# Last layers of a four-layer cross-attention stack on one Trainium2 core: rows normalised by a three-operand VectorE instruction with the reciprocal deviation as a broadcast tensor, in place of the form with two scalars

## The reference, cut to what matters

```python
def layernorm(x, scale, bias):
    m = jnp.mean(x, axis=-1, keepdims=True)
    v = jnp.mean(jnp.square(x - m), axis=-1, keepdims=True)
    return (x - m) * jax.lax.rsqrt(v + EPS) * scale + bias
ln_out = layernorm(hidden_states, ln1_s, ln1_b)
...                                   # self attention, 16 heads, masked; x = hidden + attn_out
ln_out = layernorm(x, ln2_s, ln2_b)
...                                   # cross attention over the context; x = x + cross_out
ln_out = layernorm(x, ln3_s, ln3_b)
mlp_out = gelu(ln_out @ w1 + b1) @ w2 + b2
return x + mlp_out
```

## Time and profile before

| | |
|---|---|
| median of 3 runs | 1350.19 us (1348.3 to 1353.55) |
| the profiled execution's own time | 1349.58 us |
| its span, first to last instruction | 1347.8 us |
| mean granted TensorE clock | 0.989 |
| PE busy | 1255.0 us (93%) |
| DVE busy | 840.5 us (62%) |
| ACT busy | 738.1 us (55%) |
| POOL busy | 551.7 us (41%) |

### The profile page before, as it was taken

One profiled execution on the slowest core, in us unless ns is written; L12 is line 12 of the kernel. 1 busy time (PEld: TensorE's weight loads), 2 busy tenths in 40 slices (PEclk: granted clock), 3 DMA queues, 4 the chain that ended last, 5 costly groups with the idle time before them and its releaser, 6 DMA issues.

```text
span 1347.8 us, 24724 instructions
## 1 busy us (share of the span) xinstructions
PE 1255.0 (93%) x9024; PEld 1028.4 (76%) x9024; DVE 840.5 (62%) x1892; ACT 738.1 (55%) x1986; POOL 551.7 (41%) x569
## 2 busy tenths in 40 slices
PE   6999999999987988999999999999998978888788
PEld 5777777777744556899999889999996647667667
DVE  4666666766658985666666776666667136688521
ACT  4665656566546884555555655554544344666612
POOL 3554444545349973331211322230301245687501
PEclk9999999999998998999999999999999989999999
DMA  6101010010010004021111110111001001000000
GB/s 260 50 27 52 27 52 27 30 49 27 5 65 1 1 1 149 10 72 40 48 33 48 33 48 32 48 32 48 17 1 65 2 0 55 10 1 2 1 12 20
DMA packets 15526, 50.45 MB, mean 37 GB/s; under 512 B 1840, under 2 KB 5296, under 8 KB 14384
## 3 DMA queue, kind: packets, MB, share of 16 engines
q1 hardware_dynamic: 15408, 48.87, 10.9%
HBM read 47.82 MB, written 1.05 MB: 36 GB/s over the span
## 4 chain that ended last, share of the span: by engine, by line
PE 81%; DVE 11%; ACT 3%; POOL 2%; issue 2%; DMA 0%; SPq 0%; DVEq 0%; ACTq 0%
PE pS L1477 13%; PE acc L317 6%; PE pT L1505 6%; PE acc L1557 6%; PE pC L380 5%; PE pT L367 5%; PE pS L350 4%; PE pS L1519 4%; PE acc L336 4%; PE pC L1542 4%; PE heads_scores L1298 3%; PE heads_scores L1287 3%; PE pT L1530 2%; PE acc L392 2%; DVE stats L1191 2%
## 5 line engine op out<-in xcount | busy, mean ns | idle before, releaser
L1477 PE MATMUL pS<-split_sources,split_pair_weights 128*128 128x512 f32 x768 | 213.0, 413 | 5.8 <-issue 4.3
L667 POOL TENSOR_TENSOR probs<-probs,stats 128x512 f32<-128x512 f32 x128 | 130.6, 1042 | 167.1 <-DVE stats L545 167.1
L488 ACT ACTIVATE probs<-pS,stats 128x256 f32<-128x256 f32 x256 | 118.1, 473 | 111.1 <-DVE stats L540 111.1
L1477 PEld LDWEIGHTS pS<-split_sources,split_pair_weights 128*128 128x128 f32 x768 | 136.4, 191 | 30.9 <-issue 6.6
L1654 ACT ACTIVATE probsT<-pT 128x256 f32<-128x256 f32 x128 | 49.3, 385 | 197.0 <-PE pT L1530 197.0
L1557 PE MATMUL acc<-l_wo_parts,l_ctx_parts 128*128 128x256 f32 x768 | 122.0, 295 | 1.0 <-DVE l_ctx_parts L1726 1.0
L1505 PEld LDWEIGHTS pT<-l_wv_parts,split_sources 128*128 128x128 f32 x756 | 106.9, 188 | 14.2 <-issue 2.2
L1505 PE MATMUL pT<-l_wv_parts,split_sources 128*128 128x256 f32 x756 | 110.6, 281 | 2.1 <-issue 2.1
L1780 POOL TENSOR_TENSOR split_pair_weights<-weights_a,split_pair_weights 128x1024 fp32r<-128x1024 f32 x16 | 38.1, 2382 | 170.0 <-ACT split_pair_weights L1618 169.9
L317 PE MATMUL acc<-split_sources,split_pair_weights 128*128 128x512 f32 x372 | 101.9, 408 | 1.0 <-POOL split_pair_weights L654 0.7
L1557 PEld LDWEIGHTS acc<-l_wo_parts,l_ctx_parts 128*128 128x128 f32 x768 | 99.4, 190 | 1.2 <-DVE l_ctx_parts L1726 1.2
(11 more groups left out here) (248 smaller groups left out, 2933.7 us busy)
## 6 DMA issues: line engine op xcount, KB each, us to landing
weights_a<-in_l_w SPq DMA_DIRECT2D x16, 768.5 KB, 4.3
weights_a<-in_l_w SPq DMA_DIRECT2D x16, 768.0 KB, 6.1
value_bias_rows<-in_l_bv SPq DMA_DIRECT2D x16, 256.0 KB, 4.4
weights_b<-in_l_wo SPq DMA_DIRECT2D x16, 256.0 KB, 2.6
w_fc<-in_l_w SPq DMA_DIRECT2D x4, 1024.0 KB, 5.8
bias_rows<-in_rows SPq DMA_DIRECT2D x1, 1536.0 KB, 13.0
x_residual<-in_x_dbl SPq DMA_DIRECT2D x2, 512.0 KB, 6.8
masked_scores<-in_ctx_dbl SPq DMA_DIRECT2D x2, 512.0 KB, 7.7
```

The costliest lines, as they stand in the source:

```text
L488: a = e.activation(self.E[:, n % 4, h, it, :], self.S[h][:, it, :], ACT.Exp, bias=self.st[:, 1, n % 4, h, it:it + 1], accum_out=self.st[:, ...
L667: e.tensor_tensor(self.E[:, n % 4, h, :, :], self.E[:, n % 4, h, :, :], self.st[:, 3, n % 4, h, :].unsqueeze(2).broadcast_to([P, 2, D]), A ...
L1477: mm = e.matmul(bank[:, :], self.w_qk[i % 2][kw][:, 1 - which, c, h * P:h * P + P], g.split[:, which, ks, c, half * HALF:half * HALF + HAL ...
```

## The change

The 24 instructions of line 2268 are replaced one for one. Both forms compute (x - mean) * rstd in one pass. Before, the mean and the reciprocal deviation are two per-partition scalars. After, the mean is the scalar and the reciprocal deviation is a second tensor operand: its one column, read 256 times by a step of 0. Nothing is moved: every engine has the same list in the same order, with the same waits and semaphore increments. (The new text is one line longer, so that later lines of the kernel after have numbers greater by one.)

```diff
@@ def rows(self, e, q):
         if q >= 2:
             e.wait_ge(self.h_full, q - 1)
         for i, b in enumerate((2 * c, 2 * c + 1)):
-            e.tensor_scalar(g.hn[:, 2 * (q % 2) + i, :], g.x[:, b, :], self.mv[:, b, 0:1],
-                            self.rs[:, b:b + 1], ALU.subtract, ALU.mult).then_inc(self.h, 1)
+            e.scalar_tensor_tensor(out=g.hn[:, 2 * (q % 2) + i, :], in0=g.x[:, b, :], scalar=self.mv[:, b, 0:1],
+                                   in1=self.rs[:, b:b + 1].broadcast_to([P, D]), op0=ALU.subtract,
+                                   op1=ALU.mult).then_inc(self.h, 1)
```

## The result

The changed kernel takes 1356.26 us (median of 12 runs, 1355.41 to 1361.52) against 1350.47 us (12 runs, 1348.3 to 1354.49): a ratio of 1.0052 with a 95% interval of 1.0042 to 1.0061. It is slower by 5.8 us by the medians, and by 5.7 to 8.2 us by the interval of the ratio. The forecast was 1353.0, 2.8 us slower, in a range of 1348.5 to 1357.5. The profiled execution took 1355.85 us, its span 1354.0.

The account below looks back on a forecast made before the run. The chain was PE's for 81%, with line 2268's couples on it ahead of piece T in the last stage. Couple costs summed to 2.77 us, so 1350.19 + 2.8 = 1353.0 us, range 1348.5 to 1357.5.

Parts of the forecast that it names:

- What bounds the stage: Last stage: 11 of 12 couples (two line 2268 instructions each) are on the chain to PE's transposes, piece T.
- Free cost: Line 2268 with no POOL work beside it: 478 ns against about 402, a couple 0.87 us against 0.73, +0.14 us.
- The new form is held back too: Line 2268 beside POOL: the three-operand form ends 0.28 us after POOL's instruction, the two-scalar form 0.15; +0.13 us each time.
- never held back: Rival: POOL does not hold back the new form at line 2268, every couple takes 0.87 us; -11.3 us, 1338.9 us; 7%.
- held back twice: Rival: a couple's first instruction loses its turn to a second POOL instruction, 1.27 us more in seven couples; 1361.9 us; 5%.
- no cost: Rival: the longer reading at line 2268 is made up somewhere, for instance by PE's next inputs being ready; 1350.2 us; 8%.
- The sum: Added cost of line 2268 over the last stage's couples: 0.14 + 0.60 + 0.23 + 1.80 = +2.77 us.
- POOL's delay is absorbed: POOL's own delay, 0.17 + 0.2 us in each of six couples, is hidden in its 2.48 us wait for DVE's maxima.
- speaks for neither side, and widens the range: TensorE's clock: one slow stretch of matmuls more or less is +-1.6 us, favouring neither forecast nor rivals.
- later by these amounts and nothing else: Sign of being right: each piece T starts later only by the couples' added costs.
- POOL's delay reaches the path: Rival: POOL's delay in the last stage is not hidden by its wait for maxima; +2.6 us on top, 1355.6 us; 10%.
- Will hardly tell from no change: Whole kernel: 0.2% slower, where a measurement can tell about 0.5%, 6.75 us; 84% for within 0.5%.

Follow-up runs that it names:

- the delayed kernel: Two-scalar kernel before, plus a one-column DVE copy behind each couple of line 2268 instructions, which piece T waits for: 1357.42 us, ratio 1.0064.
- filled three-operand kernel: Changed kernel plus throwaway matmuls in PE's waits, 3 ahead of piece T of couples 3 to 8 and 10, 2 ahead of projections: 1351.2 us, ratio 1.0014.
- filled two-scalar one: Kernel before plus throwaway matmuls in PE's waits, 3 ahead of piece T of couples 3 to 8 and 10, 2 ahead of projections: 1346.69 us, ratio 0.9981.

## Why the prediction was right, and where it fell short

- *What bounds the stage: right.* Each couple's step reached piece T, and piece T carried it to the end; couple 9 alone did not (its own T moved only with what lay before).
- *Free cost: right.* 475 to 479 ns, couple 0.87 us; forecast 478 and 0.87.
- *The new form is held back too: right,* shown by the couples of 1.88 us (forecast 1.87) and 2.50 us (2.54) and by the kernels without POOL's long additions, where nothing exceeds 485 ns. The rival "never held back" is gone, "held back twice" as well: the first instruction took 1090 ns, not 2.2 us. The medians of 5.8 us more rule out "no cost".
- *The sum: right to 0.2 us.* Forecast 2.77; the ledger has 2.57 (0.27 in each of the six couples, where I had 0.30, since POOL's instruction grew by 0.12 us and not by 0.17). The aside in the prediction that 133 ns for all 24 instructions would give 3.4 us does not come out: 24 x 0.133 is 3.2; 3.4 is 2.77 with 0.057 more in each of 11 couples.
- *POOL's delay is absorbed: right.* POOL waited 2.62 us for the maxima behind it, against 2.48, and DVE's wait for masks stayed 2.6 us.
- *The clock "speaks for neither side, and widens the range": wrong.* This is the term that was mis-sized, at nothing where it was 3.4 us in the profile and about 3 us in the medians (5.8 less the sum), of which 1.7 us in the profile are the stretch at 1124 us that a two-scalar kernel has too. With it the sign "later by these amounts and nothing else" failed. I had treated the slow stretches as chance of one or two either way. They are partly chance: the kernel before ran at 0.986 to 0.991. But they also answer to PE's waiting ahead of piece T, 1.37 us at couple 4 before, 1.65 after. A delay at the same place by other means brings as many stretches, and filling the waits takes away those from 1143 us on. The Trainium skill, "TensorE: Matmul & The Clock Gate" (§ HAM oscillation — how this bites in real kernels), describes a loop in which PE waits for a DMA again and again, and each wait is followed by slow matmuls. The runs here agree for waits on VectorE, with 3.0 us won by filling the kernel before and about 5 us by filling the changed one; but here not every wait is followed by a slow stretch. I had read the two clock rows and not asked what came ahead of them.
- *The range* held the time because it was made wide for single stretches; the likeliest value did not contain a systematic one. That is in part luck: 1356.26 lies outside the forecast's own 1350.5 to 1356 and nearest to the 1355.6 of the rival "POOL's delay reaches the path", which the profile rules out. From the time alone a reader would have taken the wrong rival.
- *"Will hardly tell from no change": wrong.* The interval of the ratio, 1.0042 to 1.0061, is clear of 1.

What stays open: what makes one wait bring a slow stretch and another not. Couple 5 waits 1.65 us as couple 4 does and has none behind it, and the kernel before has one behind a wait of 1.42 us (couple 7). In the changed and in the delayed kernel the waits also lie further apart than before, and no run separates their length from their place in time. How large the clock's share is in the medians is an estimate: runs of the two kernels with the same printed clock, 0.986, differ by 4.1 us (medians of 9 and of 10 runs, 1355.85 and 1351.76), more than the couples' 2.6, and one step of 0.001 in that mean is about 1.4 us. Open too: why the filled three-operand kernel keeps about one stretch more than the filled two-scalar one, and which of PE's other waits brings those at 1091 to 1108 us and at 1262. Filling was not tried there.

## What to carry to other kernels

The VectorE instruction was not freed from GpSimd by giving it a second tensor from SBUF, though that was only a broadcast column: both forms were held back. What helped was to move GpSimd's addition away from it. And where PE waits for a short chain again and again, price a lengthening of that wait twice: once as work, and once for the clock. Here each tenth of a microsecond cost more than two (5.8 us for 2.6, and 7.8 for 2.2).

## What was not expected of the hardware

- 0.2 us more ahead of each of 11 transposes, made by a one-column copy, cost 7.8 us, and the mean granted clock of the run fell from 0.989 to 0.985 or less.
- Adding matmuls whose result is thrown away made the kernel faster: 0.9981 of the time before, with 0.99 in place of 0.98 as granted clock between 1120 and 1270 us.
- The two-scalar form, when free, is not much faster than the three-operand one (402 against 478 ns), but when held back its advantage is larger, 0.13 us, and it costs POOL's next instruction next to nothing (1.33 us against 1.45).
